# An early routing gate whose scores and tables lie in PSUM, in a fused attention and mixture-of-experts kernel

## The reference

```python
scores = jax.nn.sigmoid((xf @ gate_w.T).astype(jnp.float32))
_, sel = jax.lax.top_k(scores + expert_bias[None, :], TOP_K)      # TOP_K = 2 of 8
top_scores = jnp.take_along_axis(scores, sel, axis=1) * ROUTE_SCALE
routed = xf[tok_idx] * scores_sorted[:, None]
h = jax.nn.silu(routed @ w1[e].T) * (routed @ w3[e].T)            # for each expert e
out_r = (h @ w2[e].T) * scores_sorted[:, None]
```

## Time and profile before

| | us |
|---|---|
| median of 3 runs | 1329.9 |
| lowest, highest | 1328.65, 1330.2 |
| profiled execution, span | 1324.4 |
| PE busy | 1298.5 (98%) |
| DVE busy | 916.0 (69%) |
| ACT busy | 888.2 (67%) |
| POOL busy | 1177.7 (89%) |

### The profile page before, as it was taken

One profiled execution on the slowest core, in us unless ns is written; L12 is line 12 of the kernel. 1 busy time (PEld: TensorE's weight loads), 2 busy tenths in 40 slices (PEclk: granted clock), 3 DMA queues, 4 the chain that ended last, 5 costly groups with the idle time before them and its releaser, 6 DMA issues. The chain is left out here.

```text
span 1324.4 us, 22283 instructions
## 1 busy us (share of the span) xinstructions
PE 1298.5 (98%) x8792; PEld 705.9 (53%) x8792; DVE 916.0 (69%) x1035; ACT 888.2 (67%) x1096; POOL 1177.7 (89%) x538
## 2 busy tenths in 40 slices
PE   7999999999999999999999999999999999997998
PEld 5544545454545545554545555454545555453787
DVE  6767677677766676676767676776767676868575
ACT  6666766666767667676767667666667676774464
POOL 2499999999999999999999999999999999997544
PEclk9999999999999999999999999999999999998999
DMA  7010202020100102020201102020202001000324
GB/s 209 15 35 1 49 1 49 1 49 1 41 9 9 41 2 49 1 49 1 49 2 25 25 1 49 2 49 1 49 1 49 1 11 39 1 1 23 106 73 88
DMA packets 31962, 41.55 MB, mean 31 GB/s; under 512 B 4298, under 2 KB 15186, under 8 KB 31858
## 3 DMA queue, kind: packets, MB, share of 16 engines
q1 hardware_dynamic: 31714, 40.13, 12.5%
q10 hardware_dynamic: 144, 0.00, 0.0%
HBM read 13.70 MB, written 1.11 MB: 11 GB/s over the span
## 5 line engine op out<-in xcount | busy, mean ns | idle before, releaser
L894 ACT ACTIVATE probs<-ps 128x1024 f32<-128x1024 f32 x512 | 499.1, 1033 | 77.7 <-PE ps L1324 75.0
L1055 DVE TENSOR_REDUCE peak_parts<-ps 128x2 f32<-128x1024 f32 x297 | 362.1, 1223 | 237.0 <-PE ps L1265 235.3
L1342 PE MATMUL ps<-probs,v_sb 128*64 128x512 f32 x2048 | 523.6, 607 | 0.0
L985 POOL TENSOR_TENSOR acc<-acc,probs 128x1024 f32<-128x1024 f32 x192 | 458.5, 2388 | 38.7 <-ACT probs L894 37.3
L985 POOL TENSOR_TENSOR acc_odd<-acc_odd,probs 128x1024 f32<-128x1024 f32 x192 | 460.1, 2396 | 0.0
L836 ACT COPY peak_copy<-ps 128x1024 f32<-128x1024 f32 x215 | 218.4, 1016 | 242.1 <-PE ps L1265 168.3
L1065 DVE TENSOR_REDUCE peak_parts<-peak_copy 128x2 f32<-128x1024 f32 x215 | 260.6, 1212 | 34.1 <-ACT peak_copy L836 34.1
L1342 PEld LDWEIGHTS ps<-probs,v_sb 128*64 128x64 f32 x2048 | 124.1, 136 | 157.1 <-issue 116.4
L1318 PE MATMUL ps<-q_hi,d_swap_hi 64*128 64x512 f32 x512 | 201.9, 394 | 0.4 <-ACT probs L894 0.4
L1318 PE MATMUL ps<-q_hi,d_hi 64*128 64x512 f32 x512 | 201.8, 394 | 0.1
L1324 PE MATMUL ps<-q_hi,d_lo 64*128 64x512 f32 x512 | 200.4, 392 | 0.0
(11 more groups left out here) (226 smaller groups left out, 1577.7 us busy)
## 6 DMA issues: line engine op xcount, KB each, us to landing
k_swap_hi<-k_hi SPq DMA_DIRECT2D x64, 128.0 KB, 2.3
d_swap_hi<-d_hi SPq DMA_DIRECT2D x64, 128.0 KB, 2.3
d_swap_lo<-d_lo SPq DMA_DIRECT2D x64, 128.0 KB, 2.3
q_hi<-weights_dram SPq DMA_DIRECT2D x8, 256.0 KB, 3.5
q_lo<-weights_dram SPq DMA_DIRECT2D x8, 256.0 KB, 4.9
k_hi<-weights_dram SPq DMA_DIRECT2D x8, 256.0 KB, 6.3
k_swap_hi<-weights_dram SPq DMA_DIRECT2D x8, 256.0 KB, 5.4
probs<-in_L_ffn_w_dram SPq DMA_DIRECT2D x2, 512.0 KB, 5.5
```

Of the source, the lines that this page charges most:

```text
L894: act.activation(probs[:, kt % PROBS, :], ps[:, 2 * place:2 * place + 2, :].rearrange("p a b -> p (a b)"), ACT.Exp, scale=SCALE).then_inc( ...
L985: pool.tensor_tensor(total, total, probs[:, kt % PROBS, :], ALU.add).then_inc(added, 1)
L1055: dve.tensor_reduce(peak_parts[:, :, i // STRETCHES, i % STRETCHES], ps[:, bank:bank + 2, :], AX.X, ALU.max).then_inc(peak_free, 1)
L1342: mm = pe.matmul(ps[at:at + HEAD_DIM, PV_BANK, :], v_sb[:, p, chunk_of(kt) * HEAD_DIM:(chunk_of(kt) + 1) * HEAD_DIM], probs[:, kt % PROBS, ...
```

## The change

For the first 12 blocks a function `early_gate` of its own takes the place of `gate(dve, link, 0)`. It computes the same weights in eleven instructions. `score`, a second copy of the biased scores, and the table in which equalities are found, multiplied, added up and reduced to ranks lie in PSUM, side by side in banks 6 and 7 (768 + 96 + 96 of 1024 values). The exponential and its denominator, one copy of the biased scores, `greater`, `rank`, `chosen` and the weights stay in SBUF. Each instruction with two tensor inputs reads one from PSUM and one from SBUF. The bias is added twice, once for each copy.

```diff
+        def early_gate(dve, link):
+
+            n = READY_BLOCKS
+            wide = ps[:, PEAK_BANK:PEAK_BANK + 2, :].rearrange("p a b -> p (a b)")
+            ranks = wide[:, 0:n * EXPERTS * EXPERTS].rearrange("p (b e j) -> p b e j", e=EXPERTS, j=EXPERTS)
+            at = n * EXPERTS * EXPERTS
+            score_ps, biased_ps = (wide[:, at + i * n * EXPERTS:at + (i + 1) * n * EXPERTS].rearrange(
+                "p (b e) -> p b e", e=EXPERTS) for i in range(2))
+            bias = bias_sb[:, None, :].broadcast_to([P, n, EXPERTS])
+            dve.wait_ge(tail_free, tail("logits", 0).full)
+            link(dve.tensor_scalar(gate_den[:, 0:n], gate_exp[:, 0:n], 1.0, None, ALU.add))
+            link(dve.reciprocal(score_ps, gate_den[:, 0:n]))
+            dve.tensor_tensor(biased[:, 0:n], score_ps, bias, ALU.add)
+            link(dve.tensor_tensor(biased_ps, score_ps, bias, ALU.add))
+            mine = biased[:, 0:n, :, None].broadcast_to([P, n, EXPERTS, EXPERTS])
+            other = biased_ps[:, :, None, :].broadcast_to([P, n, EXPERTS, EXPERTS])
+            link(dve.tensor_tensor(ranks, other, mine, ALU.is_equal))
+            dve.tensor_tensor(greater[:, 0:n], other, mine, ALU.is_gt)
+            link(dve.tensor_tensor(ranks, ranks, earlier[:, None, :, :].broadcast_to([P, n, EXPERTS, EXPERTS]), ALU.mult))
+            link(dve.tensor_tensor(ranks, ranks, greater[:, 0:n], ALU.add))
+            link(dve.tensor_reduce(rank[:, 0:n], ranks, AX.X, ALU.add))
+            link(dve.tensor_scalar(chosen[:, 0:n], rank[:, 0:n], 1.5, None, ALU.is_lt))
+            dve.tensor_tensor(weight_nat[:, 0:n, :], score_ps, chosen[:, 0:n], ALU.mult).then_inc(weights_ready, 1)
...
-                                    gate(dve, link, 0)
+                                    early_gate(dve, link)
```

## The result

| | before | changed |
|---|---|---|
| median of 4 runs, us | 1330.05 | 1317.98 |
| lowest, highest | 1328.65, 1330.35 | 1317.36, 1320.11 |
| ratio, 95% interval | | 0.9929, 0.9914 to 0.9944 |
| profiled span | 1324.4 | 1315.6 |

The ratio is a gain of 9.4 us (7.4 to 11.4); the spans differ by 8.8, the medians by 12.1. The ratio is not the quotient of the two medians, which is 0.991; how it is formed is not on record. The four runs of before lie high: over the 63 runs of before taken beside the experiments the median is 1328.0, the lowest 1320.2.

The account below looks back on a forecast made before the run. TensorE, busy 98% of the span, was taken as the bound, standing still for the gate. Span 1324.4 less 8.4 us (8.1 wait, 0.3 clock) is 1316.0; plus 5.5 to the median gives 1321.5 us, range 1319.3 to 1324.9.

Parts of the forecast that it names:

- The cause: TensorE's 8.1 us wait at the weights' transposes (L1297) for VectorE's gate, slowed by alternating with GpSimd's adds, would vanish.
- The gate's length: VectorE's early gate would run from 1195.68 to about 1204.1 us instead of 1213.81, with `chosen` waiting for GpSimd's third add.
- The slack in front of TensorE: Weights ready early enough for TensorE to start at 1204.2 us, while it comes only at 1205.8: 1.6 us to spare.
- The late low parts of w3: Four VectorE instructions L1154 beside adds: at most 10.9 us, to 1218.9, likely ending near 1213; needed at 1221.1, so hidden.
- The last add: GpSimd's last add would end near 1228.9 us, ahead of L1355, which needs it at 1230.9: hidden.
- The gain behind the wait: At the weights' transposes, 0.3 us from TensorE's clock staying at its upper level; ScalarE's DMA wait takes any further clock gain.
- a gain of up to 9.3 for a shorter round trip: Upper case of the gain, 9.3 instead of 8.4 us, if ScalarE's DMA round trip is shorter than before.
- The absolute time: Whole kernel: span 1316.0 us plus the 5.5 by which the median 1329.9 lay above the profiled span, giving 1321.5.
- The rivals: Gate still late, 0.07; DMA takes the wait's place, 0.05; change does not do what it says, 0.03; slower, 0.02.
- Gate still late: At the early gate, `chosen` loses another add or tables take 1.5 us: 1322.3, up to 1324.9 us; chance 0.07.
- The rule of the Trainium skill on a larger fixed part from PSUM: VectorE's fixed part: 58 cycles from SBUF, 120 from PSUM; would add 0.5 us to the gate, total unmoved.
- The prediction's 1204.6 for this case: Time in us when the weights would be ready if PSUM's larger fixed part added 0.5 us; still ahead of TensorE.

Follow-up runs that it names:

- small_adds: Kernel before with its SBUF gate, but GpSimd's adds in the last unit from the third on take 8 columns, not 1024; median 1316.52 us, ratio 0.9909.
- warm_wait: Kernel before, with eight matmuls that nobody reads run on TensorE ahead of the weights' transposes; median 1325.48 us, ratio 0.9984.
- both_psum: Changed kernel, with a PSUM operand also in both tensor_scalars of the early gate and the late gate moved to bank 5; median 1315.98 us, ratio 0.9918.
- warm_longer: Kernel before, with eleven matmuls that nobody reads run on TensorE ahead of the weights' transposes; 1325.17 us, one run.
- before_again: Kernel before, unchanged, run and profiled a second time; median 1328.34 us, profiled span 1328.3.
- two_back: Changed kernel with two of the four table instructions reading two SBUF tensors again; median 1321.48 us, ratio 0.9950.
- three_back: Changed kernel with three of the four table instructions, all but `greater`, reading two SBUF tensors again; median 1324.52 us, ratio 0.9980.
- two_back_again: Second profile of the changed kernel with two table instructions back on two SBUF inputs; span 1323.6 us.

## Why the prediction was right, and where it was not

**The cause** was right: TensorE's 8.1 us wait for the gate, gone in all three profiles of the changed kernel. The earlier trace rows carried it: a duration that never stretches never waits. The tables took 0.96 to 0.97 us (predicted 0.98), the doubled bias add 0.26 each, the tensor_scalar ended right behind an add, and TensorE began the transposes at once. By small_adds, sharing with GpSimd is the whole of the slowness.

**The gate's length** was predicted at 8.4 us (1195.7 to 1204.1) and was 8.1. It started 1.1 us earlier, at 1194.54, since L576 did not wait for an add in this execution; that is chance and not the change. The add that `chosen` waited for ended at 1202.28, not at 1203.65. The slack in front of TensorE, counted as in the prediction, was 3.9 us, predicted 1.6. The 2.3 more is luck: 1.4 of it is how the adds fell, 0.9 that TensorE came later, at 1206.7.

**The late low parts of w3** (L1154, now L1178) took 5.9 + 2.5 us beside adds, as bounded from the earlier trace rows, and ended near 1214.9, ahead of the 1220.6 at which TensorE needs them. I had them end near 1213 in a pause of GpSimd at 1211; that pause did not come: the exponentials started at 1210.00 already. Hidden all the same. The last add ended at 1228.95, L1379 started at 1230.41: hidden, as said.

**The gain behind the wait** was set too small: 0.3 us for the clock, because ScalarE's wait for the DMA, 4.14 us from first to third copy in the earlier trace rows, was taken to hold up the exponential and to swallow the rest. It took 2.14 or 2.15 us in eleven of the fourteen profiles, the three of the changed kernel among them, 2.8 in warm_wait and 3.9 in both_psum: the one row I had was the longest. The term measured 1.6 us; warm_longer, and before_again with its short round trip, show that it is the clock. I had named a gain of up to 9.3 for a shorter round trip; from R to F it was 9.9.

**The absolute time.** Against the runs of before the forecast was close: 8.4 us of gain where the ratio says 9.4 (7.4 to 11.4). As a time it was off: the measured median of 1317.98 is 3.5 us under the 1321.5 and 1.3 under the lower end of the range, 1319.3. The step was the last of the sum, "the median of the runs is 1329.9, 5.5 above the profiled span, and that part stands". The 1329.9 came from three runs and is 1.9 us above the median of the 63 later ones. And the 5.5 mixed two things. In all runs on record the time is 1.75 to 1.85 us above its own span, except for two runs of warm_wait with 2.0 and 2.6. So the profiled execution of before corresponds to 1326.2 us and was a short one; the other 3.7 of the 5.5 were scatter of before. The gain was then read from that short execution, with a wait of 8.1 where before_again had 10.1. With 1.8 the same sum, 1316.0 + 1.8, gives 1317.8. That it meets the measured median so closely is partly luck: its gain is 1.5 us short of the 9.9 from R to F, while R came 1.0 us later.

**The rivals.** None of the four occurred. "Gate still late" came true only in two_back and three_back, where I provoked it. The rule of the Trainium skill on a larger fixed part from PSUM ("VectorE: DVE Perf Modes", TRN2 errata) is again not seen: the table with one PSUM input took 0.96 to 0.97 us in the changed kernel and 0.95 to 0.96 from SBUF in small_adds, a difference of 0.01 where 62 cycles more, an estimate from that page, would be 0.06. The prediction's 1204.6 for this case is a slip in its sum: there `chosen` waits for the add that ends at 1203.65 with or without the longer fixed parts, so most of the 0.5 us would be hidden. Nothing hangs on it.

**The scatter of before** (1320.2 to 1330.4 over its runs, against 1316.2 to 1320.1 for ten runs of the changed kernel) I had not thought of. Two parts of it are seen in the traces. One is the early drop, 1.2 to 3.5 us, whatever the kernel. The other is the gate: in all thirteen profiles with L576 ahead of the gate, L576 waited where GpSimd's second add had started before it and not otherwise (by 0.02 us in both_psum it did not). How early the add starts goes with TensorE's clock behind the logits; no run sets that clock on purpose, so this link is read from the order of events and not tested. In all five profiles without the drop behind the logits and with L576 ahead of the gate, L576 took 2.9 us and the first tensor_scalar 2.4; in seven of those with a drop (5.0 to 6.0 us in the table) 0.7 and 0.2 to 0.25; the first profile of before lies between (2.8 and 0.2). So an execution that is faster at the logits is slower at the gate. The two drops shut each other out here: none of the five profiles with the early drop has one behind the logits, and eight of the nine others do. The three slowest runs of the changed kernel (1319.25 to 1320.11) show a mean clock of 0.996 to 0.997, the seven others 0.999 (1316.2 to 1318.6); that they are early drops is likely, but none was profiled. What decides on either drop stays open, as does what became of the lowest runs of before near 1320 us, none of which was profiled.

## What to carry to other kernels

Look at how the durations of one instruction form spread: a form whose time jumps by about the length of a neighbour engine's instruction waits for that neighbour, and where it ends tells for which. Putting one of two inputs in an idle PSUM bank costs nothing per element here and takes VectorE out of GpSimd's way; single-input tensor_scalars between SBUF tensors need it too. Add to a span only what lies around that same execution, never the distance to a median of others, and profile a kernel more than once before its one trace prices a wait.

## What the runs showed of the hardware

- A VectorE instruction with two SBUF inputs waits until GpSimd's add under way has ended, and the next add waits for it: 0.96 us alone, about 3.0 beside adds of 2.4, which stretch to 3.05 to 3.11. With one input in PSUM it took 0.96 to 0.97 beside the same adds. The Trainium skill says this in "SBUF — State Buffer", in the section on who interferes with whom; the traces agree.
- A tensor_scalar over 128x96 from SBUF to SBUF waits too (1.46 us, 2.37, or 0.20 alone); with its input in PSUM 0.26, with its output there 0.25, beside adds. The same section states it for the two-port modes; agreed.
- TensorE, after standing still for 5.1 us (two_back_again), 8.1 (before) or 10.1 (before_again), ran the next 3 to 6 us mostly at a granted clock of 0.50, the 1.2 GHz level; 9.7 us of matmuls nobody reads in that place kept it at 1.00, the 2.4 GHz level. Eight of them and a pause of 2.9 us did not: the scores behind took 0.79 and 0.62 us in place of 0.50 and 0.39.
- The same 24 logits matmuls, 2.85 us with TensorE busy throughout, were followed by a clock of 0.52 for 3.5 us in the changed kernel's profile and of 1.00 in that of before_again. The windows behind those matmuls, before_again first:

```profile
1192.60:1196.00 3.40, 3.40 (x21) 1.52 (x20) 3.40 (x3) 2.67 (x4) 2.57 (x2) 1.00 0.00 0
```

And the changed kernel:

```profile
1190.50:1194.00 3.50, 3.50 (x15) 2.11 (x16) 3.50 (x4) 2.29 (x4) 2.16 (x1) 0.52 0.00 0
```
